# A mixture-of-experts stage: two-way softmax by tanh, router operands in PSUM, weight transposes one step later

## The chip, the cores and the metric

One core of one Trainium2 chip runs the whole kernel as one program. The metric is device time in microseconds (us) of one execution. Before the change the median of three runs is 1157.18 us (1154.05 to 1157.69).

## What is computed

The input `x` is 8 sequences of 512 tokens with 128 features, in fp32. Attention with 16 heads comes first, then a mixture of 8 experts of which each token uses 2.

```
x = layernorm(x + (x + attention(x)))
logits = x @ gate_w                              # 8 per token
top, idx = top_k(logits, 2); w = softmax(top)    # ties: the lower index wins
combine = w at idx, 0 elsewhere
h = silu(x @ w1[e]); y = h @ w2[e]
x = layernorm(x + sum over e of combine[e] * y[e])
```

## The kernel before

Every large product keeps fp32 accuracy by splitting each operand into a rounded high part and a low remainder, and adding three products (`product`: high by high, high by low, low by high).

The program is written out by hand, engine by engine: each engine has one list of instructions in a fixed order, and semaphores (`wait_ge`) tie the lists together. An engine that waits holds up all that stands behind it in its list. The attention stage is some 840 us of the span. The change lies in the expert stage behind it.

**Expert stage.** It goes through 8 sequences b ("chunks"), each with 8 steps, one per expert e; k is 8b+e. Features lie on the partitions, the 512 tokens of a sequence along the free dimension. In step e the engines do this:

- PE (TensorE): `hidden(k+3)`, 6 matmuls of 512 columns into a PSUM bank pair; `second(k)`, 6 more (L710, L714), which accumulate over the 8 experts in PSUM bank Y; `spread_c(k+3)`, one matmul (L700) that copies the routing weight of expert e over all partitions into bank CB. In step 0 the spread stands ahead of the second product. So a step is 13 matmuls.
- ACT (ScalarE): `silu_part(k+3)` (L912), then `g_hi_part(k+2)` (L919), the high part of the gated hidden values.
- DVE (VectorE): `gate_part(k+3)` (L1175), silu times the spread weight. PE's next spread waits for it, because there is one CB bank.
- POOL (GpSimd): `g_lo_part(k+2)` (L402), the low part, a subtraction of two SBUF tiles of 128x1024. `gate_part` of two steps later waits for it.

**Routing of the next sequence** runs in between. `route` (three matmuls, step 0) gives transposed logits, `logits_to_tokens` (four transposes, step 1) turns them. `route1` on DVE then copies the 32 logits of each partition (L1104), takes the maximum, subtracts it (L1109), and counts for each expert how many logits are above it, ties broken by index (L1112 to L1122). ACT takes the exponential (`exp_part`, L894). `route2` on DVE masks, sums, divides (L1128 to L1136) and so makes `combine`. `transpose_c` on PE (L681, step 3) waits for it; then ACT and DVE split the result (`cT_part`), and the first spread of the next sequence, in step 5, waits for that. All tiles of `route1` and `route2` are in SBUF but the source of the first copy.

**Normalizations.** The first one of sequence b+2 goes `to_tokens` (PE, L654, step 4), `stats1` (DVE, L1078, L1082, step 4), `rstd_part` (POOL, L396 and L398, step 5), `norm1` (DVE, L1092, step 6), `transpose_x1` (PE, L660, step 7), `x1T_part`. The second one, of sequence b-1, is `sum_part` (DVE, step 0, ahead of that step's gate): two additions over 128x512 (L1184, L1186), of which the first frees bank Y for `second` of the new sequence. Then come `sum_to_tokens` (PE, L723, step 2), `stats2_part` (DVE, step 2), `rstd_part`, and `norm2` (DVE, L1196, step 4). The first normalization works in PSUM bank NA (6), the second in NB (7), and the logits are in NB too:

```
        def nb(b):
            return COARSE + 1 if is_first(b) else NB
```

The first two and the last two chunks are written out; the four between run in a loop of two chunks.

## Time and profile before

| what | value |
|---|---|
| median of 3 runs (lowest, highest) | 1157.18 us (1154.05, 1157.69) |
| the profiled execution | 1155.28 us |
| its span, first to last instruction | 1153.5 us |
| busy share of the span | PE 92%, DVE 74%, POOL 63%, ACT 50% |
| mean granted clock of TensorE | 0.965 of 2.4 GHz |

All rows come from the one profiled execution, so costs are added against its own 1155.28 us (a span of 1153.5 and 1.8 around it). It lies 1.90 us below the median. Busy shares are means over two stages with different limits. The stage that is changed begins at about 842 us, where attention ends, and its own waits are read there. In the rows a tile has the name of the buffer that it is carved from: `probs_even` holds the small routing and normalization tiles, `x_tok` silu and gated values, `q_pair` and `k_pair` the high and low parts, `v` the transposed logits and the summed output.

### The profile page before, as it was taken

How to read it: one execution, taken by the hardware profiler on the slowest of the kernel's cores; microseconds unless marked ns; L12 is line 12 of the kernel's file. 1: busy time of each engine (PE TensorE's matmuls, PEld its weight loads, DVE VectorE, ACT ScalarE, POOL GpSimd, SP SyncE). 2: the span in 40 equal slices, each digit the busy share in tenths (PEclk: the TensorE clock that was granted, in tenths of full speed). 3: DMA queues.
4: the chain of work that ended last, by engine and by line, in shares of the span. 5: the costliest groups of instructions: out<-in, count | busy, mean ns of one | idle time of the engine just before them, and what ended most of it. 6: DMA issues, size and time to landing. Idle time of an engine off the chain costs nothing. (4 is left out here: it accounts for less than half of the span.)

```text
span 1153.5 us, 18564 instructions
## 1 busy us (share of the span) xinstructions
PE 1061.5 (92%) x5912; PEld 647.3 (56%) x5912; DVE 852.7 (74%) x1172; ACT 575.0 (50%) x680; POOL 727.1 (63%) x376
## 2 busy tenths in 40 slices
PE   4999899999999999999999999999957888889886
PEld 2555445555555555555555555556525666667664
DVE  4786778778878877877877887787735677776774
ACT  4554445455455454545545545444414565665563
POOL 0486656676666666667667666766745655666665
PEclk8899999999999999999999999999988899999999
DMA  7203012111111111111211111111000000000000
GB/s 182 78 20 110 19 42 78 46 45 59 45 45 61 62 45 45 59 45 45 77 45 45 59 46 45 50 73 46 33 27 10 10 19 12 8 18 18 9 10 19
DMA packets 41326, 52.31 MB, mean 45 GB/s; under 512 B 9296, under 2 KB 27728, under 8 KB 41296
## 3 DMA queue, kind: packets, MB, share of 16 engines
q1 hardware_dynamic: 41296, 51.92, 12.9%
q8 instruction: 17, 0.28, 0.1%
q14 instruction: 13, 0.11, 0.0%
HBM read 6.30 MB, written 2.10 MB: 7 GB/s over the span
## 5 line engine op out<-in xcount | busy, mean ns | idle before, releaser
L976 DVE TENSOR_REDUCE neg_max<-psum 128x2 fp32r<-128x1024 f32 x256 | 310.7, 1214 | 69.5 <-PE psum L507 67.0
L537 PE MATMUL psum<-q_pair,k_pair 64*128 64x512 f32 x1536 | 221.7, 393 | 3.3 <-DVE xT L958 1.9
L402 POOL TENSOR_TENSOR k_pair<-x_tok,q_pair 128x1024 fp32r<-128x1024 f32 x64 | 152.2, 2388 | 91.2 <-ACT q_pair L919 91.2
L367 POOL TENSOR_TENSOR probs_sum<-probs_sum,x_tok 128x1024 f32<-128x1024 f32 x64 | 152.6, 2384 | 72.3 <-ACT x_tok L824 69.3
L367 POOL TENSOR_TENSOR probs_sum<-probs_sum,probs_even 128x1024 f32<-128x1024 f32 x64 | 152.8, 2387 | 70.0 <-ACT probs_even L824 66.3
L824 ACT ACTIVATE probs_even<-psum 128x1024 f32<-128x1024 f32 x128 | 127.9, 1024 | 112.4 <-PE psum L543 112.4
L824 ACT ACTIVATE x_tok<-psum 128x1024 f32<-128x1024 f32 x128 | 128.3, 1025 | 110.1 <-PE psum L543 110.1
L537 PEld LDWEIGHTS psum<-q_pair,k_pair 64*128 64x128 f32 x1536 | 145.7, 186 | 32.5 <-DVE xT L958 2.4
L1175 DVE TENSOR_TENSOR x_tok<-x_tok,psum 128x1024 f32<-128x1024 f32 x64 | 77.9, 1217 | 78.2 <-PE psum L700 48.6
L555 PE MATMUL psum<-x_tok,v 128*64 128x512 f32 x512 | 132.5, 628 | 0.0
L555 PE MATMUL psum<-probs_even,v 128*64 128x512 f32 x512 | 128.4, 611 | 0.0
L507 PE MATMUL psum<-k_pair,q_pair 64*128 64x512 f32 x512 | 116.6, 450 | 10.2 <-DVE neg_max L976 10.2
L367 POOL TENSOR_TENSOR probs_sum<-probs_even 128x1024 f32<-128x1024 f32 x32 | 75.8, 2369 | 73.8 <-ACT probs_even L824 37.2
L371 POOL TENSOR_TENSOR zT_lo<-zT,zT_hi 128x512 fp32r<-128x512 f32 x64 | 83.5, 1305 | 44.7 <-ACT zT_hi L831 44.7
L1008 DVE TENSOR_TENSOR zT<-psum,zT 128x512 f32<-128x512 f32 x64 | 44.3, 692 | 87.8 <-PE psum L555 87.8
L367 POOL TENSOR_TENSOR probs_sum<-x_tok 128x1024 f32<-128x1024 f32 x32 | 75.8, 2369 | 49.0 <-DVE group_sums L992 45.8
L543 PE MATMUL psum<-shift,ones_r 64*128 64x512 f32 x512 | 102.0, 393 | 0.0
L507 PEld LDWEIGHTS psum<-k_pair,q_pair 64*128 64x128 f32 x512 | 48.6, 185 | 92.6 <-issue 54.1
L912 ACT ACTIVATE x_tok<-psum 128x1024 f32<-128x1024 f32 x64 | 65.5, 1025 | 58.0 <-PE psum L457 55.6
L831 ACT ACTIVATE zT_hi<-zT 128x512 fp32r<-128x512 f32 x64 | 40.5, 633 | 106.3 <-PE psum L457 106.2
L992 DVE TRANSPOSE_TENSOR_REDUCE group_sums<-probs_sum 128x32 f32<-128x1024 f32 x64 | 79.0, 1235 | 0.2 <-POOL probs_sum L367 0.2
L710 PE MATMUL psum<-q_pair,w_tab 128*128 128x512 f32 x256 | 72.3, 405 | 1.0 <-DVE v L1184 0.7
(117 smaller groups left out, 1836.7 us busy)
## 6 DMA issues: line engine op xcount, KB each, us to landing
xT_cur<-xT SPq DMA_DIRECT2D x32, 512.0 KB, 2.9
wqk_cur<-w_tab SPq DMA_DIRECT2D x62, 256.0 KB, 2.6
wo_cur<-w_tab SPq DMA_DIRECT2D x64, 128.0 KB, 2.0
x_tok<-L_attn_x_dram SPq DMA_DIRECT2D x8, 256.0 KB, 5.2
probs_even<-acc SPq DMA_DIRECT2D x8, 256.0 KB, 2.3
out_dram<-probs_even SPq DMA_DIRECT2D x8, 256.0 KB, 2.3
acc<-L_ffn_w_dram SPq DMA_DIRECT2D x1, 1024.0 KB, 5.7
acc<-L_attn_w_q_dram SPq DMA_DIRECT2D x1, 512.0 KB, 5.1
```

The source lines that it names most:

```text
L367: nc.gpsimd.tensor_tensor(probs_sum[:], left, probs[j][:, :, c, :], ALU.add).then_inc(s["added"], 1)
L371: nc.gpsimd.tensor_tensor(zT_lo[:], zT[:], bits(zT_hi[:]), ALU.subtract).then_inc(s["zT_lo_done"], 1)
L402: nc.gpsimd.tensor_tensor(g_lo[e % GB], gated[e % 2], bits(g_hi[e % GB]), ALU.subtract).then_inc(s["g_lo_done"], 1)
L507: mm = nc.tensor.matmul(psum[:, COARSE + h, :], q_pair[u][half, 0, t * P:(t + 1) * P], k_pair[u][half, 0, :], start=True, stop=True)
L537: nc.tensor.matmul(psum[:, 2 * (t % 2) + h, :], k_pair[u][half, kp, keys], q_pair[u][half, qp, :], start=(kp == 0 and qp == 0), stop=False)
L543: mm = nc.tensor.matmul(psum[:, 2 * (t % 2) + h, :], ones_r[half, :], shift[half].rearrange("p t q -> p (t q)"), start=False, stop=True)
L555: mm = nc.tensor.matmul(psum[h * DK:(h + 1) * DK, Z, :], v[u // 2][:, u % 2, c, h, :], probs[u % 2][:, h, c, :], start=(c == 0), stop=(c = ...
L710: nc.tensor.matmul(psum[:, Y, :], w2_tab[:, e, f, part, :], g_hi[e % GB][:, f, :], start=(e == 0 and f == 0 and part == 0), stop=False)
L824: nc.scalar.activation(probs[j][:, :, t, :], psum[:, 2 * (t % 2):2 * (t % 2) + 2, :], ACT.Exp).then_inc(s["exp_done"], 1)
L976: nc.vector.tensor_reduce(neg_max[:].rearrange("p (h k) -> p h k", h=2)[:, :, t], psum[:, COARSE:COARSE + 2, :], AX.X, ALU.max, negate=Tru ...
L992: nc.vector.tensor_reduce(group_sums[:], probs_sum[:].rearrange("p h (c i) -> p (h c) i", i=BLK), AX.X, ALU.add, apply_transpose=True).the ...
L1175: nc.vector.tensor_tensor(gated[e % 2], silu[e % 2], psum[:, CB, :].unsqueeze(1).broadcast_to([P, FC, S]), ALU.mult).then_inc(s["gated"], 1)
```

## The change

- The softmax over two chosen logits becomes `0.5 * (1 + tanh(own - (sum of both) / 2))`, and the factor 0.5 is applied where the transposed weights are split (`cT_part`). The maximum, the subtraction, the exponential, the sum of weights, the reciprocal and the division go. A mask, a sum of the two chosen logits and one combined operation (`middle`) come. ACT computes tanh.
- Logits, tie flags, counts and the tanh lie in PSUM (`log_bank`), so that no routing operation on DVE, except reductions, reads only from SBUF. The logits' bank is now NA.
- `route2` is split. Its main part stands ahead of `gate_part(5)` on DVE, the last multiplication (`route3`) behind it.
- `transpose_c` and `cT_part` go from step 3 to step 4, `to_tokens` and `stats1` from 4 to 5, `stats2_part` from 2 to 3, `norm2` from 4 to 7.
- The first addition of `sum_part` writes to bank Y itself; `second` of the new sequence now waits for `sum_done`, the end of both additions, and no longer for `sum_half`.

```diff
@@ -153,7 +153,12 @@
             return COARSE if is_first(b) else NA
         def nb(b):
-            return COARSE + 1 if is_first(b) else NB
+            return COARSE + 1 if is_first(b) else NA
+        def log_bank(b):
+            tiles = psum[:, nb(b), :].rearrange("p (t m) -> p t m", t=TT)
+            return [tiles[:, :, i * NE:(i + 1) * NE] for i in range(3)] + [tiles[:, :, NE * NE:2 * NE * NE]]
         names = """x0_in x_near_in x_far_in w_in ident_set ones_set zeroed w_split gate_split
@@ -664,8 +669,6 @@
                 pe.wait_ge(s["x1T_hi_done"], b + 1)
                 pe.wait_ge(s["x1T_lo_done"], b + 1)
-                wait(pe, s["norm2_done"], TT * (b - 2))
                 product(psum[:, nb(b), :], [gate_tab[:, 0, :], gate_tab[:, 1, :]],
                         [xT[:, b, 0, :], xT[:, b, 1, :]]).then_inc(s["logitT_done"], 1)
@@ -703,7 +706,7 @@
             def second(k, b, e):
                 if e == 0:
-                    wait(pe, s["sum_half"], b)
+                    wait(pe, s["sum_done"], b)
                 pe.wait_ge(s["g_hi_done"], k + 1)
                 for f in range(FC):
                     for part in range(2):
@@ -718,7 +721,9 @@
             def sum_to_tokens(b):
                 pe.wait_ge(s["sum_done"], b + 1)
-                wait(pe, s["logit_out"], b + 3 if not past(b, 2) else B)
+                pe.wait_ge(s["z_done"], PAIRS)
+                wait(pe, s["norm2_done"], TT * b)
                 for t in range(TT):
                     mm = nc.tensor.transpose(psum[:, NB, t * P:(t + 1) * P], sum_tok[:, t * P:(t + 1) * P], ident[:])
                 mm.then_inc(s["sum_tok_done"], 1)
@@ -768,12 +773,12 @@
                             route(b + 1)
                         if e == 1:
                             logits_to_tokens(b + 1)
-                        if e == 3:
+                        if e == 4:
                             transpose_c(b + 1)
                     if e == 2 and not is_first(b):
                         sum_to_tokens(b - 1)
                     if not past(b, 2):
-                        if e == 4:
+                        if e == 5:
                             to_tokens(b + 2)
                         if e == 7:
                             transpose_x1(b + 2)
@@ -889,21 +894,22 @@
                 wait(act, s["logit_done"], b)
                 nc.scalar.activation(logitT, psum[:, nb(b), :], ACT.Copy).then_inc(s["logitT_out"], 1)
-            def exp_part(b):
-                act.wait_ge(s["shifted"], b + 1)
-                nc.scalar.activation(expl[:], shifted[:], ACT.Exp).then_inc(s["exp_logit"], 1)
+            def tanh_part(b):
+                act.wait_ge(s["middle_done"], b + 1)
+                nc.scalar.activation(log_bank(b)[2], middle[:], ACT.Tanh).then_inc(s["tanh_done"], 1)
             def cT_part(b, j):
                 act.wait_ge(s["cT_done"], b + 1)
                 wait(act, s["cb_done"], NE * (b - 1))
-                nc.scalar.activation(cT[0:NE, j, :], psum[0:NE, na(b), :], ACT.Copy).then_inc(s["cT_hi_done"], 1)
+                nc.scalar.activation(cT[0:NE, j, :], psum[0:NE, na(b), :], ACT.Copy, scale=0.5).then_inc(s["cT_hi_done"], 1)
             zT_part(PAIRS - 2)
             x1T_part(0)
             zT_part(PAIRS - 1)
             logitT_part(0)
-            exp_part(0)
+            tanh_part(0)
             def silu_part(k, e):
                 act.wait_ge(s["h_done"], k + 1)
@@ -937,9 +943,9 @@
                     if not past(b, 1):
                         if e == 0:
                             logitT_part(b + 1)
-                        if e == 1:
-                            exp_part(b + 1)
-                        if e == 3:
+                        if e == 2:
+                            tanh_part(b + 1)
+                        if e == 4:
                             cT_part(b + 1, 1 - j)
                     if e == 7 and not past(b, 2):
                         x1T_part(b + 2)
@@ -1099,51 +1105,52 @@
             def route1(b):
+                logits, over, _, ties = log_bank(b)
+                ties = ties.rearrange("p t (a b) -> p t a b", a=NE)
                 dve.wait_ge(s["logit_done"], b + 1)
                 wait(dve, s["c_done"], b)
-                nc.vector.tensor_copy(logit[:], psum[:, nb(b), :].rearrange("p (t m) -> p t m", t=TT)[:, :, 0:NE]
-                                      ).then_inc(s["logit_out"], 1)
+                nc.vector.tensor_copy(logit[:], logits).then_inc(s["logit_out"], 1)
                 dve.wait_ge(s["logit_out"], b + 1)
-                nc.vector.tensor_reduce(top[:], logit[:], AX.X, ALU.max).then_inc(s["route_step"], 1)
-                dve.wait_ge(s["route_step"], ROUTE * b + 1)
-                nc.vector.tensor_tensor(shifted[:], logit[:], over_experts(top), ALU.subtract).then_inc(s["shifted"], 1)
-                other, own = logit[:].unsqueeze(2), logit[:].unsqueeze(3)
+                other, own = logits.unsqueeze(2), logit[:].unsqueeze(3)
                 shape = [P, TT, NE, NE]
                 nc.vector.tensor_tensor(above[:], other.broadcast_to(shape), own.broadcast_to(shape),
                                         ALU.is_gt).then_inc(s["route_step"], 1)
-                nc.vector.tensor_tensor(tied[:], other.broadcast_to(shape), own.broadcast_to(shape),
+                nc.vector.tensor_tensor(ties, other.broadcast_to(shape), own.broadcast_to(shape),
                                         ALU.is_equal).then_inc(s["route_step"], 1)
+                dve.wait_ge(s["route_step"], ROUTE * b + 2)
+                nc.vector.tensor_tensor(ties, ties, before.unsqueeze(1).broadcast_to(shape),
+                                        ALU.mult).then_inc(s["route_step"], 1)
                 dve.wait_ge(s["route_step"], ROUTE * b + 3)
-                nc.vector.tensor_tensor(tied[:], tied[:], before.unsqueeze(1).broadcast_to(shape),
-                                        ALU.mult).then_inc(s["route_step"], 1)
+                nc.vector.tensor_tensor(above[:], ties, above[:], ALU.add).then_inc(s["route_step"], 1)
                 dve.wait_ge(s["route_step"], ROUTE * b + 4)
-                nc.vector.tensor_tensor(above[:], above[:], tied[:], ALU.add).then_inc(s["route_step"], 1)
+                nc.vector.tensor_reduce(over, above[:], AX.X, ALU.add).then_inc(s["route_step"], 1)
+            def route2(b):
+                logits, over, _, _ = log_bank(b)
                 dve.wait_ge(s["route_step"], ROUTE * b + 5)
-                nc.vector.tensor_reduce(chosen[:], above[:], AX.X, ALU.add).then_inc(s["route_step"], 1)
-            def route2(b):
-                dve.wait_ge(s["route_step"], ROUTE * b + 6)
-                dve.wait_ge(s["exp_logit"], b + 1)
-                nc.vector.scalar_tensor_tensor(weight[:], chosen[:], 2.0, expl[:], ALU.is_lt,
+                nc.vector.scalar_tensor_tensor(picked[:], over, 2.0, logit[:], ALU.is_lt,
                                                ALU.mult).then_inc(s["route_step"], 1)
+                nc.vector.tensor_scalar(mask[:], over, 2.0, None, ALU.is_lt).then_inc(s["route_step"], 1)
                 dve.wait_ge(s["route_step"], ROUTE * b + 7)
-                nc.vector.tensor_reduce(wsum[:], weight[:], AX.X, ALU.add).then_inc(s["route_step"], 1)
+                nc.vector.tensor_reduce(both[:], picked[:], AX.X, ALU.add).then_inc(s["route_step"], 1)
                 dve.wait_ge(s["route_step"], ROUTE * b + 8)
-                nc.vector.reciprocal(rwsum[:], wsum[:]).then_inc(s["route_step"], 1)
-                dve.wait_ge(s["route_step"], ROUTE * b + 9)
+                nc.vector.scalar_tensor_tensor(middle[:], both[:].unsqueeze(2).broadcast_to([P, TT, NE]), -0.5, logits,
+                                               ALU.mult, ALU.add).then_inc(s["middle_done"], 1)
+            def route3(b):
+                dve.wait_ge(s["tanh_done"], b + 1)
+                dve.wait_ge(s["route_step"], ROUTE * b + 7)
                 wait(dve, s["cT_done"], b)
-                nc.vector.tensor_tensor(combine[:], weight[:], over_experts(rwsum), ALU.mult).then_inc(s["c_done"], 1)
-            ROUTE = 9
-            def over_experts(v):
-                return v[:].unsqueeze(2).broadcast_to([P, TT, NE])
+                nc.vector.scalar_tensor_tensor(combine[:], log_bank(b)[2], 1.0, mask[:], ALU.add,
+                                               ALU.mult).then_inc(s["c_done"], 1)
+            ROUTE = 8
             def cT_part(b, j):
                 dve.wait_ge(s["cT_hi_done"], b + 1)
-                nc.vector.tensor_tensor(cT[CLO:CLO + NE, j, :], psum[0:NE, na(b), :], bits(cT[0:NE, j, :]),
-                                        ALU.subtract).then_inc(s["cT_lo_done"], 1)
+                nc.vector.scalar_tensor_tensor(cT[CLO:CLO + NE, j, :], psum[0:NE, na(b), :], 0.5, bits(cT[0:NE, j, :]),
+                                               ALU.mult, ALU.subtract).then_inc(s["cT_lo_done"], 1)
             dve.wait_ge(s["gate_in"], DMA)
@@ -1166,6 +1173,7 @@
             route1(0)
             route2(0)
             stats1(1)
+            route3(0)
             def gate_part(k, e):
                 dve.wait_ge(s["silu_done"], k + 1)
@@ -1181,9 +1189,9 @@
                 dve.wait_ge(s["y_done"], NE * (b + 1))
                 wait(dve, s["sum_tok_done"], b)
-                nc.vector.tensor_tensor(sum_tok, psum[:, Y, :], bits(xT[:, b, 0, :]), ALU.add).then_inc(s["sum_half"], 1)
+                nc.vector.tensor_tensor(psum[:, Y, :], psum[:, Y, :], bits(xT[:, b, 0, :]), ALU.add).then_inc(s["sum_half"], 1)
                 dve.wait_ge(s["sum_half"], b + 1)
-                nc.vector.tensor_tensor(sum_tok, sum_tok, bits(xT[:, b, 1, :]), ALU.add).then_inc(s["sum_done"], 1)
+                nc.vector.tensor_tensor(sum_tok, psum[:, Y, :], bits(xT[:, b, 1, :]), ALU.add).then_inc(s["sum_done"], 1)
             def stats2_part(b):
                 norm_stats(NB, stats2, mv2, b, "sum_tok_done", "stats2_done", "mv2_done", ("norm2_done", TT))
@@ -1210,22 +1218,24 @@
                         sum_part(b - 1)
                         if not past(b, 1):
                             x1T_part(b + 1)
+                    if not past(b, 1) and e == 2:
+                        route2(b + 1)
                     if not last_step(b, e + 3):
                         gate_part(b * NE + e + 3, (e + 3) % NE)
                     if not past(b, 1):
                         if e == 1:
                             route1(b + 1)
                         if e == 2:
-                            route2(b + 1)
-                        if e == 3:
+                            route3(b + 1)
+                        if e == 4:
                             cT_part(b + 1, 1 - j)
                     if not is_first(b):
-                        if e == 2:
+                        if e == 3:
                             stats2_part(b - 1)
-                        if e == 4:
+                        if e == 7:
                             norm2(b - 1)
                     if not past(b, 2):
-                        if e == 4:
+                        if e == 5:
                             stats1(b + 2)
                         if e == 6:
                             norm1(b + 2)
```

DVE, second chunk, from the last operation of `route1` (step 1) to the gate behind the split of the weights. L1175 is `gate_part`, L1145 `cT_part`, L1078 and L1082 the statistics. Before:

```order
L1122 TENSOR_REDUCE probs_even<-probs_even 128x32
L1175 TENSOR_TENSOR x_tok<-x_tok,psum 128x1024
L1128 SCALAR_TENSOR_TENSOR probs_even<-probs_even 128x32
L1131 TENSOR_REDUCE probs_even<-probs_even 128x4
L1133 RECIPROCAL probs_even<-probs_even 128x4
L1136 TENSOR_TENSOR probs_even<-probs_even 128x32
L1078 BN_STATS probs_even<-psum 128x6 x4
L1082 BN_AGGR probs_even<-probs_even 128x2 x4
L1175 TENSOR_TENSOR x_tok<-x_tok,psum 128x1024
L1145 TENSOR_TENSOR xT_cur<-psum,xT_cur 8x512
```

The same place in the changed kernel (L1183 is `gate_part`, L1152 `cT_part`, L1145 `route3`, L1084 and L1088 the statistics):

```order
L1126 TENSOR_REDUCE psum<-probs_even 128x4x8
L1132 SCALAR_TENSOR_TENSOR probs_even<-psum,probs_even 128x32
L1134 TENSOR_SCALAR probs_even<-psum 128x32
L1136 TENSOR_REDUCE probs_even<-probs_even 128x4
L1138 SCALAR_TENSOR_TENSOR probs_even<-probs_even,psum 128x32
L1183 TENSOR_TENSOR x_tok<-x_tok,psum 128x1024
L1145 SCALAR_TENSOR_TENSOR probs_even<-psum,probs_even 128x32
L1183 TENSOR_TENSOR x_tok<-x_tok,psum 128x1024
L1084 BN_STATS probs_even<-psum 128x6 x4
L1088 BN_AGGR probs_even<-probs_even 128x2 x4
L1183 TENSOR_TENSOR x_tok<-x_tok,psum 128x1024
L1152 SCALAR_TENSOR_TENSOR xT_cur<-psum,xT_cur 8x512
```

Four small operations moved ahead of the gate of step 2, one stays behind it, and the statistics and the weight split each stand one gate later.

DVE, in the loop, from the gates of steps 6 and 7 to the sum of the finished sequence in step 0 of the next chunk (L1092 is `norm1`; L1184 and L1186 are the two additions). Before:

```order
L1175 TENSOR_TENSOR x_tok<-x_tok,psum 128x1024
L1088 ISA
L1092 TENSOR_SCALAR probs_even<-psum,probs_even 128x128 x4
L1171 REGISTER_ALU
L1175 TENSOR_TENSOR x_tok<-x_tok,psum 128x1024
L1181 REGISTER_ALU
L1184 ISA
L1184 TENSOR_TENSOR v<-psum,xT 128x512
L1186 ISA
L1186 TENSOR_TENSOR v<-v,xT 128x512
```

And now (L1098 is `norm1`, L1204 `norm2`, L1192 and L1194 the additions):

```order
L1098 TENSOR_SCALAR probs_even<-psum,probs_even 128x128 x4
L1179 REGISTER_ALU
L1183 TENSOR_TENSOR x_tok<-x_tok,psum 128x1024
L1200 ISA
L184 REGISTER_ALU
L1204 TENSOR_SCALAR probs_even<-psum,probs_even 128x128 x4
L1192 ISA
L1192 TENSOR_TENSOR psum<-psum,xT 128x512
L1194 ISA
L1194 TENSOR_TENSOR v<-psum,xT 128x512
```

The four operations of the second normalization now stand between the last gate of a chunk and the two additions.

ACT, second chunk, around the exponential (L894) and the tanh (L899). Before, and then now:

```order
L912 ACTIVATE x_tok<-psum 128x1024
L919 ACTIVATE q_pair<-x_tok 128x1024
L894 ACT_TABLE_LOAD
L894 ACTIVATE probs_even<-probs_even 128x32
L912 ACT_TABLE_LOAD
```

```order
L918 ACTIVATE x_tok<-psum 128x1024
L925 ACTIVATE q_pair<-x_tok 128x1024
L899 ACTIVATE psum<-probs_even 128x4x8
L918 ACTIVATE x_tok<-psum 128x1024
L925 ACTIVATE q_pair<-x_tok 128x1024
```

The two table loads around the exponential have gone, and none stands at the tanh, which comes one step later.

## Rows read from the trace of the kernel before

**Rows 1.** The page, section 2: granted clock in 40 equal slices
```profile
PEclk8899999999999999999999999999988899999999
```
**Rows 2.** Waits from 825 us to the end (us in total, times, longest)
```profile
PE psum L681 <- DVE probs_even L1136: 28.8, 8, 4.0
```
**Rows 3.** Timeline of PE: start, us, line, operands, count, [idle before <-releaser]
```profile
950.58 0.60 PE L660 MATMUL psum<-ident,probs_even 128*128 128x128 f32 x4
...
952.71 0.50 PE L700 MATMUL psum<-xT_cur,w_tab 128*128 128x512 f32 x1
953.38 1.19 PE L710 MATMUL psum<-q_pair,w_tab 128*128 128x512 f32 x4 [0.18 <-DVE v L1184]
...
958.97 0.60 PE L675 MATMUL psum<-ident,v 128*128 128x128 f32 x4
...
962.41 0.60 PE L723 MATMUL psum<-ident,v 128*128 128x128 f32 x4
...
970.42 0.69 PE L681 MATMUL psum<-ident,probs_even 128*8 128x128 f32 x4 [3.97 <-DVE probs_even L1136]
...
975.45 0.60 PE L654 MATMUL psum<-ident,probs_even 128*128 128x128 f32 x4
...
1087.87 0.60 PE L660 MATMUL psum<-ident,probs_even 128*128 128x128 f32 x4
```
**Rows 4.** Timeline of DVE, routing of one chunk
```profile
960.46 0.18 DVE L1104 COPY probs_even<-psum 128x32 f32<-128x32 f32 x1
...
964.67 1.22 DVE L1175 TENSOR_TENSOR x_tok<-x_tok,psum 128x1024 f32<-128x1024 f32 x1 [0.59 <-ACT x_tok L912]
965.81 2.25 DVE L1128 SCALAR_TENSOR_TENSOR probs_even<-probs_even 128x32 f32<-128x32 f32 x1
...
968.53 1.83 DVE L1136 TENSOR_TENSOR probs_even<-probs_even 128x32 f32<-128x32 f32 x1
```
**Rows 5.** Timeline of POOL at the same time
```profile
965.67 4.65 POOL L402 TENSOR_TENSOR k_pair<-x_tok,q_pair 128x1024 fp32r<-128x1024 f32 x2 [3.67 <-ACT q_pair L919]
```
**Rows 6.** Line L1128, all eight: ns min/median/max
```profile
L1128 DVE SCALAR_TENSOR_TENSOR probs_even<-probs_even x8: 193/2257/2264, 871.0 to 1102.8; 128x32 f32<-128x32 f32 x8
```
**Rows 7.** Busy time and granted clock (after the five engines' columns) in four stretches
```profile
93.50:97.00 3.50, 3.50 (x13) 1.74 (x13) 0.00 (x0) 1.97 (x2) 0.63 (x1) 0.51 0.00 0
...
148.00:151.50 3.50, 3.50 (x14) 0.98 (x12) 3.02 (x5) 0.60 (x1) 2.35 (x1) 0.53 0.00 0
...
936.00:941.00 5.00, 4.92 (x17) 3.92 (x18) 2.99 (x11) 2.41 (x3) 1.20 (x2) 0.66 0.00 0
941.00:950.00 9.00, 9.00 (x43) 7.32 (x42) 6.97 (x19) 4.95 (x6) 7.08 (x5) 1.00 0.19 60
```
**Rows 8.** Groups by line and form from 840 us: the table loads ahead of silu
```profile
L912 ACT ACT_TABLE_LOAD x8 | 10.3, 1283 | 0.1
```
**Rows 9.** Timeline of DVE: second normalization of a chunk, and the chunk's end
```profile
942.48 1.36 DVE L1196 TENSOR_SCALAR probs_even<-psum,probs_even 128x128 f32<-128x128 f32 x4
...
951.43 1.22 DVE L1175 TENSOR_TENSOR x_tok<-x_tok,psum 128x1024 f32<-128x1024 f32 x1 [1.10 <-POOL k_pair L402]
952.57 0.68 DVE L1184 TENSOR_TENSOR v<-psum,xT 128x512 f32<-128x512 f32 x1
953.40 0.80 DVE L1186 TENSOR_TENSOR v<-v,xT 128x512 f32<-128x512 f32 x1
```
**Rows 10.** Timeline of PE: three shorter idle stretches in the attention stage
```profile
92.60 0.39 PE L455 MATMUL psum<-w_tab,xT_cur 128*128 128x256 f32 x1 [2.46 <-DMA xT_cur<-xT]
...
117.55 0.96 PE L537 MATMUL psum<-q_pair,k_pair 64*128 64x512 f32 x6 [1.27 <-DVE recip L998]
...
146.72 0.50 PE L507 MATMUL psum<-k_pair,q_pair 64*128 64x512 f32 x2 [2.30 <-DVE neg_max L976]
```
**Rows 11.** Timeline of PE: the weight transposes of the first sequence
```profile
871.95 0.60 PE L681 MATMUL psum<-ident,probs_even 128*8 128x128 f32 x4 [0.93 <-DVE probs_even L1136]
```
**Rows 12.** Timeline of DVE: statistics of the second sequence, just behind its weights
```profile
871.81 0.88 DVE L1078 BATCH_NORM_STATS2 probs_even<-psum 128x6 f32<-128x128 f32 x4
```

8 lines of the change are left out of this document (4 added, 4 removed).

## The prediction

> **What bounds the kernel now.** I read the granted clock by slices first [rows 1]. It is at its upper level through attention and falls at the start and around the expert stage, so TensorE loses something there. Attention is not touched by the change; everything is decided in the last 310 us. The waits of that stage name one culprit: PE waits 8 times at the transposes of the routing weights (L681), 28.8 us in all, for DVE's last routing operation (L1136) [rows 2]. Seven of these are alike, near 4 us each; the first one is 0.93 us [rows 11], so the seven hold 27.9 us.
>
> The timeline of PE shows one of them [rows 3]. From the transposes at 958.97 to those at 962.41 are 3.44 us, and that is one full step with its four transposes and next to no waiting. From 962.41 to 970.42, with the same content, are 8.01 us, and from 970.42 to 975.45 are 5.03 us. The first excess, 4.57 us, is the wait (3.97) and a short one ahead of it; the second, 1.59 us, has no idle time. There the clock is low: 0.66 as a mean in the matching stretch of the chunk before, and 1.00 right behind it [rows 7], which are the 1.2 and 2.4 GHz levels mixed. So each wait costs a chunk of 34.3 us (four of them between 950.58 and 1087.87 [rows 3]) 4.57 + 1.59 = **6.16 us**. No other engine sets a chunk: POOL needs 8 products of 2.4 us and some 2.5 us more.
>
> Why is DVE late? L1128 works on 32 elements per partition and takes 2.25 us, and L1136 takes 1.83 [rows 4]. Over all eight, L1128 ranges from 193 to 2264 ns [rows 6]. The long ones lie beside POOL's two subtractions, 965.67 to 970.32 [rows 5], and end as a POOL operation ends: 965.81 + 2.25 is 968.06, 968.53 + 1.83 is 970.36. Both read two tiles in SBUF. The gate (L1175), also beside them elsewhere, reads one tile in SBUF and one in PSUM and keeps 1.22 us.
>
> **The change, part by part.**
>
> *The weights come in time.* Before, `route1` and the wait behind it fill 960.46 to 964.67, of which 0.59 is a wait for ACT [rows 4]; so `route1` is at most 3.6 us, and it loses two operations of eight. The four operations that now stand ahead of the gate are priced by the shortest L1128, 0.19 us, with the gaps 0.22 each: 0.9 us [rows 6]. The gate then starts between 963.8 and 965.0, against 964.67 before: 0.9 earlier to 0.3 later. The last operation stands behind it and needs 0.2, if it doesn't wait for POOL: `combine` is ready by 966.4. The transposes, now one step later, want it at about 966.2 + 3.4 = 969.6. More than 3 us of slack, so both excesses go, in seven chunks: 7 x 6.16 = **43.1 us gained**. What is late next in this chain is the split of the weights, ahead of the first spread of the next sequence: ACT 0.6 and DVE 0.7 behind the transposes, with a whole hidden and second product (2.8) before the spread wants it. I cost it at nothing.
>
> *Table loads.* The order shows 14 of them gone behind the first silu, of 1283 ns each [rows 8]. They made the 0.59 us wait of the gate [rows 4], which is in the 4.57 already. ACT otherwise idles for PE. Nothing more is gained.
>
> *PSUM operands.* As a source, PSUM costs DVE nothing here: L1184 with one source in PSUM takes 0.68 us, L1186 with both in SBUF 0.80 [rows 9]. As a destination of DVE it has no row. Below, it can't gain over the bare time. Above, if it doubled the operation, three operations of `route1` (some 0.4 each, of which about 0.5 is covered by the slack of the gate) and the first addition (0.7) would cost 0.7 + 0.7 us a chunk, 10 us in all. The nearest row is the 0.68 of a PSUM source; I take 0 and keep 10 for the upper end.
>
> *The sum at the chunk's end.* This is what the change pays with. Before, the last gate of a chunk starts at 951.43, the first addition follows at 952.57, and `second` of the new sequence starts at 953.38, 1.95 us after the gate's start [rows 3, 9]. Now `norm2` stands between, four operations that take 1.3 us in a row (1.36 [rows 9]), and `second` waits for both additions, 0.7 more. It starts 1.95 + 1.3 + 0.7 = 3.95 us after the gate's start. The gate itself waited 1.10 us in all for POOL [rows 9], whose reciprocal root stands in the same place still; 0 to 1.1 could be won, I take 0.4, and 0.3 more since the low part of the first normalization, for which PE waits behind `second`, is then done. That is 2.0 - 0.4 - 0.3 = 1.3 us at five boundaries, 2.0 at the last one (no POOL wait there), and 0.3 at the first, where no `norm2` stands yet: 5 x 1.3 + 2.0 + 0.3 = **8.8 us lost**.
>
> *The clock at that place.* PE's spread ends by 952.6 to 952.9 (it starts at 952.71 at the latest [rows 3]), and `second` would start at 951.43 - 0.4 + 3.95 = 955.0. PE is idle for 2.1 to 2.4 us at six boundaries. The trace has two stretches like it: 2.46 and 2.30 us idle [rows 10]. PE resumed at full clock both times, and 1 us later the clock fell: 0.51 in 93.5 to 97.0 and 0.53 in 148.0 to 151.5 [rows 7]. An idle stretch of 1.27 us [rows 10] was followed by matmuls at their usual rate. Each fall costs half of 3.5 us, 1.7, and PE is what bounds the chunk: 6 x 1.7 = **10.2 us lost**. The Trainium skill, "TensorE: Matmul & The Clock Gate", section "Why this matters for your kernels", advises to keep idle gaps below about 3 us and takes the clock to last through shorter ones. These rows speak against it; by the skill this term would be 0 and the time 10.2 us shorter.
>
> *The first sequence.* There its `combine` is finished behind the statistics of the second one, which take 0.88 us and their four aggregates; before, they stood behind [rows 12]. `route1` gets shorter too. Between 0.93 us won (that wait gone [rows 11]) and 1.3 lost, I take **0.8 lost**, as the statistics alone cost 0.88.
>
> *The tail.* `norm2` of the last but one sequence moves by three steps in which DVE has only gates, and POOL's last products still set the end. Nothing.
>
> *Sum:* 43.1 - 8.8 - 10.2 - 0.8 = 23.3 us. Against the profiled execution's 1155.28 us this gives 1132.0. The median of before is 1.9 us above it, the lowest run 1.2 below, so I keep **1132 us**.
>
> **The rivals.**
>
> 1. *The clock stays up at the boundary.* It is the skill's rule of the paragraph above, and rows of 1.27 us idle time [rows 10] show it for shorter stretches. A gate that starts earlier than I take would help it. Against it stand two out of two stretches of 2.3 and 2.5 us. Then the gain is 33.5 and the time 1122 us. Chance 0.18.
> 2. *No stall at the boundary at all*, if the last gate came so much earlier that `norm2` and the additions fit. They need 3.95 us after the gate, and PE has 1.2 us of spread and slack; it speaks strongly against. Gain 42, time 1113 us. Chance 0.04.
> 3. *PSUM destinations are dear.* Up to 10 us as worked out, 1142 us. Nothing in the rows speaks for it but that no row shows the operation. Chance 0.13.
> 4. *Slower than before: the routing block ahead of the gate.* Ten small operations now stand in front of `gate_part` of step 2, and PE's next spread waits for that gate. It has about 0.5 us of slack. If the block were X longer than that, PE would lose X in seven chunks and, from 2 us on, 1.7 more by the clock. To eat 23.3 us and pass the 0.3% it takes 27 = 7 x (X + 1.7), so X above 2.1 us: each of the ten operations 0.26 us longer than now. The bare 193 ns of L1128 [rows 6] speak against it. At X = 3 the time would be 1132 + 33 = 1165 us. Chance 0.03.
> 5. *Something else holds the chunk at 34 us*, so that the wait was hidden. The step from 958.97 to 962.41 takes 3.44 us without it, and POOL's load is below 22 us a chunk. About 1155 us; chance 0.03. That the change doesn't do what it says is excluded for the table loads and the order of DVE, which are read from the program; that PSUM sources keep DVE clear of POOL is shown by the gate.
>
> **How the numbers follow.** The forecast, 1132, has 0.59. Its own range is 1126 to 1138: the gate's start (0.4 between 0 and 1.1 at six boundaries, about 4 us), the first sequence (1 to 2 us), and one or two clock falls more or less. The range reaches to rival 1 with its own few us and most of the way to rival 3: **1118 to 1141 us**. A measurement tells this kernel from no change at about 0.3%, 3.5 us. Faster by more than that: 0.94; within it: 0.03; slower: 0.03.
>
> **What would show it.** In the new profile no wait of PE at the transposes of the weights, and the routing operations at their bare 0.2 and 0.4 us beside POOL. Chunks of 31 to 31.5 us. Seven waits of PE at `second` for DVE's second addition, six of 2.1 to 2.4 us, each followed by some 3.5 us at half clock. If chunks take 29.5 and the clock is at 1.00 in them, rival 1 is right; if they take 28 or less and that wait is missing, rival 2; if DVE's operations into PSUM last 0.8 us, rival 3. A wait of PE at the spread of step 3 for the gate, of over a microsecond, would be rival 4.

## The result, and the profile after the change

| | before | changed |
|---|---|---|
| median | 1156.33 us (1154.05 to 1157.69, 4 runs) | 1127.24 us (1123.37 to 1129.15, 4 runs) |
| the profiled execution | 1155.28 us | 1129.15 us |
| its span | 1153.5 us | 1127.4 us |
| mean granted clock of TensorE | 0.965 | 0.975 |

The ratio is 0.9746, with a 95% interval of 0.9715 to 0.9778: 29 us faster. The changed kernel's profiled execution is its slowest one, 1.9 us above its median, as before's lay 1 us below. A second set of runs, beside two of the experiments, gave 0.9787 (0.9771 to 0.9804), so the gain is 24 to 29 us. One of the four runs of the kernel with the exponential, below, took 1679 us at a mean granted clock of 0.565 and is left out of its median.

The waits of the expert stage first, in the view that [rows 2] come from, here from 825 us to the end of the changed kernel (us in total, times, longest):

```profile
PE psum L713 <- DVE v L1194: 14.2, 7, 2.3
...
PEld psum L684 <- DVE probs_even L1145: 1.8, 1, 1.8
...
PE psum L684 <- DVE probs_even L1145: 1.6, 1, 1.6
```

The seven waits of 4 us at the transposes of the weights (now L684) are gone, and the first sequence's alone is left (1.6 us). In their place PE waits seven times at the first matmul of `second` (L713) for DVE's second addition (L1194), 14.2 us in all: six of 2.1 to 2.3 us and, at the first boundary, one of 0.83. The timeline of PE, start and duration in us, shows one chunk with two of these boundaries; these rows answer to [rows 3]:

```profile
938.54 0.39 PE L703 MATMUL psum<-xT_cur,w_tab 128*128 128x512 f32 x1
941.22 1.18 PE L713 MATMUL psum<-q_pair,w_tab 128*128 128x512 f32 x4 [2.29 <-DVE v L1194]
...
957.91 0.60 PE L684 MATMUL psum<-ident,probs_even 128*8 128x128 f32 x4
...
961.35 0.60 PE L659 MATMUL psum<-ident,probs_even 128*128 128x128 f32 x4
...
972.34 1.43 PE L713 MATMUL psum<-q_pair,w_tab 128*128 128x512 f32 x4 [2.29 <-DVE v L1194]
```

From 957.91 to 961.35 are 3.44 us, where the same content took 5.03 before. From 941.22 to 972.34 is one chunk: 31.12 us, before 34.3. The clock, in the view of [rows 7] (the granted clock stands behind the five engines' columns):

```profile
930.00:941.00 11.00, 8.93 (x43) 6.98 (x41) 8.61 (x21) 7.31 (x8) 9.07 (x7) 1.00 0.03 10
941.00:942.00 1.00, 0.79 (x3) 0.67 (x4) 1.00 (x3) 0.00 (x0) 1.00 (x1) 1.00 0.87 288
942.50:946.00 3.50, 3.50 (x10) 2.75 (x9) 0.31 (x1) 0.60 (x1) 0.75 (x1) 0.53 0.02 5
946.00:957.00 11.00, 11.00 (x54) 8.96 (x53) 7.21 (x18) 6.66 (x8) 6.30 (x3) 1.00 0.01 1
```

Here PE resumes at 2.4 GHz (granted clock 1.00 up to 942), and within a microsecond or so it falls to 1.2 GHz for about 3.5 us. At 1034.58 and 1065.46 the clock is at 0.50 already when PE resumes. DVE around the routing block, the same view as [rows 4]:

```profile
949.47 0.18 DVE L1112 COPY probs_even<-psum 128x32 f32<-128x32 f32 x1
949.69 0.42 DVE L1116 TENSOR_TENSOR probs_even<-psum,probs_even 128x256 f32<-128x256 f32 x1
950.03 0.42 DVE L1118 TENSOR_TENSOR psum<-psum,probs_even 128x256 f32<-128x256 f32 x1
...
951.42 0.43 DVE L1126 TENSOR_REDUCE psum<-probs_even 128x32 f32<-128x256 f32 x1
951.88 0.19 DVE L1132 SCALAR_TENSOR_TENSOR probs_even<-psum,probs_even 128x32 f32<-128x32 f32 x1
...
952.20 0.19 DVE L1136 TENSOR_REDUCE probs_even<-probs_even 128x4 f32<-128x32 f32 x1
952.42 0.19 DVE L1138 SCALAR_TENSOR_TENSOR probs_even<-probs_even,psum 128x32 f32<-128x32 f32 x1
952.62 1.22 DVE L1183 TENSOR_TENSOR x_tok<-x_tok,psum 128x1024 f32<-128x1024 f32 x1
953.76 0.18 DVE L1145 SCALAR_TENSOR_TENSOR probs_even<-psum,probs_even 128x32 f32<-128x32 f32 x1
```

POOL's subtractions run from 948.60 to 951.01 and from 952.05 to 954.45 beside most of them, and none is longer for it: not those with one source in PSUM, and not the reduction L1136 (0.19 us), which reads one tile only, in SBUF. A PSUM destination costs nothing: L1118 writes to PSUM and takes 0.42, as L1116, which writes to SBUF. And the boundary, the view of [rows 9]:

```profile
937.14 1.22 DVE L1183 TENSOR_TENSOR x_tok<-x_tok,psum 128x1024 f32<-128x1024 f32 x1 [0.69 <-POOL k_pair L407]
938.28 1.36 DVE L1204 TENSOR_SCALAR probs_even<-psum,probs_even 128x128 f32<-128x128 f32 x4
939.56 0.69 DVE L1192 TENSOR_TENSOR psum<-psum,xT 128x512 f32<-128x512 f32 x1
940.39 0.69 DVE L1194 TENSOR_TENSOR v<-psum,xT 128x512 f32<-128x512 f32 x1
```

`second` starts at 941.22, 4.08 us after the gate's start at 937.14 (forecast: 3.95). The four rows are, in order, what PE waits for: the gate, the normalization, and the two additions.

### The profile page after: what moved, and what is told of

It is laid out like the page before. It is cut to its first block, busy times and chain, and to the rows that moved or that the text cites. A ratio compares the mean times of both kernels' runs of the same rounds, so it can differ in the third digit from the quotient of the medians.

```text
span 1127.4 us, 18513 instructions
## 1 busy us (share of the span) xinstructions
PE 1053.1 (93%) x5912; PEld 647.2 (57%) x5912; DVE 816.1 (72%) x1164; ACT 557.6 (49%) x666; POOL 727.9 (65%) x376
## 4 chain that ended last, share of the span: by engine, by line
PE 76%; POOL 10%; issue 6%; DVE 4%; ACT 1%; DMA 1%; SPq 1%; POOLq 0%; DVEq 0%; ACTq 0%
PE psum L560 21%; PE psum L542 15%; PE psum L460 9%; POOL k_pair L407 8%; PE psum L512 7%; PE psum L461 6%; PE psum L462 6%; PE psum L548 5%; PE psum L713 2%; PE psum L520 1%; PE psum L717 1%; POOL probs_even L403 1%; DMA xT_cur<-xT 1%; DVE neg_max L982 1%; PE psum L574 0%
## 5 line engine op out<-in xcount | busy, mean ns | idle before, releaser
L1183 DVE TENSOR_TENSOR x_tok<-x_tok,psum 128x1024 f32<-128x1024 f32 x64 | 78.1, 1220 | 88.1 <-PE psum L703 68.2
L713 PE MATMUL psum<-q_pair,w_tab 128*128 128x512 f32 x256 | 73.9, 412 | 14.2 <-DVE v L1194 14.2
```

The lines of the kernel that those rows point to most:

```text
L713: nc.tensor.matmul(psum[:, Y, :], w2_tab[:, e, f, part, :], g_hi[e % GB][:, f, :], start=(e == 0 and f == 0 and part == 0), stop=False)
```

## The experiments

Each ratio is to the kernel before, run beside it on the same chip, with its 95% interval. "The changed kernel" has 0.9746 and 0.9787 in its two sets. The change made three things at once: operands in PSUM, a softmax by tanh, and a new order with a new wait. They are taken apart here.

### What the boundary costs: norm2 in step 4 again

In DVE's list, of the changed kernel:

```diff
                     if not is_first(b):
                         if e == 3:
                             stats2_part(b - 1)
-                        if e == 7:
+                        if e == 4:
                             norm2(b - 1)
```

> The changed kernel with norm2 back in step 4, so that it no longer stands between a chunk's last gate and the two additions. My theory (the additions come late because of norm2, PE idles 2.3 us, and the clock falls behind it): PE's idle time at the second product of a new sequence shrinks by 1.3 us, from 2.3 to 1.0 us, the clock no longer falls there, and six boundaries give 6 x (1.3 + 1.7) = 18 us: about 1109 us. Rival A (the clock falls there for another reason than this stretch): 6 x 1.3 = 8 us, about 1119 us, with the half-clock stretches still there. Rival B (DVE or POOL is what spaces the chunk, the time comes back elsewhere): under 3 us.

Measured: ratio 0.9625 (0.9605 to 0.9646), median 1111.18 us, 14 to 19 us faster than the changed kernel. PE at three boundaries:

```profile
939.86 1.19 PE L713 MATMUL psum<-q_pair,w_tab 128*128 128x512 f32 x4 [1.02 <-DVE v L1194]
...
968.13 1.20 PE L713 MATMUL psum<-q_pair,w_tab 128*128 128x512 f32 x4 [1.03 <-DVE v L1194]
...
996.39 1.19 PE L713 MATMUL psum<-q_pair,w_tab 128*128 128x512 f32 x4 [1.00 <-DVE v L1194]
```

The idle stretch is 1.0 us, a chunk 28.27 us. That is 2.85 us less, of which 1.27 is idle time; the other 1.58 has no idle time ahead of it. The clock shows it, which is 1.00 over 100 us of this kernel (the view of [rows 7]):

```profile
900.00:1000.00 100.00, 96.11 (x448) 77.01 (x447) 70.36 (x162) 62.51 (x70) 77.22 (x43) 1.00 0.06 19
```

So both terms of the forecast's loss are real: without the long stretch its idle time and the half clock behind it are both gone. Rivals A and B fall. The changed kernel's second trace (`changed_again`, below) gives the price of a fall without any edit. There the clock fell at five of the six boundaries, and at one it did not:

```profile
940.01 1.19 PE L713 MATMUL psum<-q_pair,w_tab 128*128 128x512 f32 x4 [2.27 <-DVE v L1194]
...
969.54 1.37 PE L713 MATMUL psum<-q_pair,w_tab 128*128 128x512 f32 x4 [2.29 <-DVE v L1194]
```

```profile
940.00:950.00 10.00, 9.99 (x47) 8.21 (x48) 5.81 (x14) 4.68 (x6) 5.18 (x3) 1.00 0.12 39
...
970.50:974.00 3.50, 3.50 (x10) 2.69 (x10) 0.64 (x1) 0.60 (x1) 1.07 (x1) 0.53 0.07 28
```

The chunk without the fall is 29.53 us, the next one, with it, 31.14 (969.54 to 1000.68): 1.6 us, at the same idle time.

### The same from the other side: the sum as it was

```diff
-                    wait(pe, s["sum_done"], b)
+                    wait(pe, s["sum_half"], b)
...
-                nc.vector.tensor_tensor(psum[:, Y, :], psum[:, Y, :], bits(xT[:, b, 0, :]), ALU.add).then_inc(s["sum_half"], 1)
+                nc.vector.tensor_tensor(sum_tok, psum[:, Y, :], bits(xT[:, b, 0, :]), ALU.add).then_inc(s["sum_half"], 1)
                 dve.wait_ge(s["sum_half"], b + 1)
-                nc.vector.tensor_tensor(sum_tok, psum[:, Y, :], bits(xT[:, b, 1, :]), ALU.add).then_inc(s["sum_done"], 1)
+                nc.vector.tensor_tensor(sum_tok, sum_tok, bits(xT[:, b, 1, :]), ALU.add).then_inc(s["sum_done"], 1)
```

> The changed kernel with the sum as it was before: the first addition writes to SBUF and frees the PSUM bank, the second product waits for it alone; norm2 stays in step 7. Theory: the idle stretch shrinks by 0.7 us, from 2.3 to 1.6 us, at six boundaries and from 0.8 to 0.1 at the first: 5 us, about 1122 us, if the clock still falls behind 1.6 us; if it stays up, 10 us more, about 1112 us. Rival: the second addition, now of two SBUF tiles again, waits for POOL and delays x1T_part and the gate behind it, so that the gain is under 2 us.

Measured: ratio 0.9651 (0.9632 to 0.9669), median 1113.63 us. The boundary of two chunks:

```profile
937.42 1.19 PE L713 MATMUL psum<-q_pair,w_tab 128*128 128x512 f32 x4 [1.46 <-DVE v L1192]
...
966.29 1.19 PE L713 MATMUL psum<-q_pair,w_tab 128*128 128x512 f32 x4 [1.46 <-DVE v L1192]
```

The stretch is 1.46 us and a chunk 28.87 us; the clock is 1.00 from 900 to 1000 us. It is 0.83 us less idle time and 1.42 us less besides. An edit that is worth 0.8 us a chunk on DVE gave 2.25, because no fall of the clock followed the shorter stretch at any of the six boundaries.

### Both

> The changed kernel with both: norm2 in step 4 and the second product waiting for the first addition alone. Theory: the idle stretch goes from 2.3 to 0.3 us, the clock stays up, six boundaries give 6 x (2.0 + 1.7) = 22 us and the first 0.7: about 1105 us. Rival (once the stretch is short enough for the clock, the rest is hidden): no better than norm2 early alone.

Measured: ratio 0.9611 (0.9593 to 0.963), median 1109.48 us, 2 us better than norm2 early alone. The theory's 1105 was too good, and the timeline of PE shows a good part of why:

```profile
937.58 1.20 PE L713 MATMUL psum<-q_pair,w_tab 128*128 128x512 f32 x4 [0.18 <-DVE v L1192]
939.62 0.49 PE L460 MATMUL psum<-xT,wqk_cur 128*128 x1 [0.38 <-DVE xT L1103]
...
965.65 1.19 PE L713 MATMUL psum<-q_pair,w_tab 128*128 128x512 f32 x4 [0.18 <-DVE v L1192]
```

The wait at `second` is down to 0.18 us, but a new one of 0.38 us stands right behind it, at `route`, for the low part of the first normalization (`x1T_part`, L1103), which DVE does after both additions. A chunk is 28.07 us, 0.20 less than with norm2 early alone, where 0.84 of idle time had gone. So 0.38 of the 0.64 us that are missing is this wait, which had been hidden behind the first one; the other 0.26 has no idle time that the trace shows.

### And x1T_part between the two additions

```diff
                 nc.vector.tensor_tensor(sum_tok, psum[:, Y, :], bits(xT[:, b, 0, :]), ALU.add).then_inc(s["sum_half"], 1)
+                between()
                 dve.wait_ge(s["sum_half"], b + 1)
...
-                        sum_part(b - 1)
-                        if not past(b, 1):
-                            x1T_part(b + 1)
+                        if past(b, 1):
+                            sum_part(b - 1)
+                        else:
+                            sum_part(b - 1, lambda: x1T_part(b + 1))
```

> The kernel with norm2 early and the second product waiting for the first addition, with the low part of the first normalization (x1T_part) put between the two additions. Theory: PE's remaining wait behind the second product (0.36 us for x1T_part, some 0.3 more until matmuls run on) goes, 0.3 to 0.6 us in six chunks: 2 to 4 us less than the 1109 of both_early. Rival (the second addition, of two SBUF tiles, then meets POOL and delays the gate): no gain.

Measured: ratio 0.959 (0.957 to 0.961), median 1106.95 us, the lowest of the study. Its interval is clear of the kernel before's and the changed one's, but overlaps that of the last section (0.9593 to 0.963), so it is the chunk that shows the gain. PE's transposes of the sum, once a chunk, come every 27.4 us:

```profile
948.20 0.60 PE L728 MATMUL psum<-ident,v 128*128 128x128 f32 x4
...
975.64 0.60 PE L728 MATMUL psum<-ident,v 128*128 128x128 f32 x4
```

That is 0.63 us a chunk (28.07 to 27.44) below the kernel of the last section, at the upper end of what was expected. By my estimate a chunk without any wait needs 27.0 us: 8 steps of 3.02 us (954.89 to 957.91 of the changed kernel), five sets of transposes at 0.42 (3.44 less 3.02) and the three matmuls of `route`, 0.7. So little is left.

### The operands back in SBUF

Of the changed kernel, its order, tanh and waits kept:

```diff
         def log_bank(b):
-            tiles = psum[:, nb(b), :].rearrange("p (t m) -> p t m", t=TT)
-            return [tiles[:, :, i * NE:(i + 1) * NE] for i in range(3)] + [tiles[:, :, NE * NE:2 * NE * NE]]
+            return sb_bank
...
+        sb_bank = [logit[:], carve(TT, NE), carve(TT, NE), carve(TT, NE * NE)]
```

> The changed kernel with logits, flags, counts and tanh in SBUF again, the transposes in step 4. Theory: the operations with two SBUF sources wait for POOL's subtraction again. In the block ahead of the gate of step 2 that costs 1 to 4 us, the gate comes late, PE waits for it at the spread and not at the transposes, 0.5 to 3.5 us a chunk and a clock fall with the longer ones: ratio to before 0.98 to 1.00. Rival (the order is what counts, the transposes have 3 us of slack in step 4): ratio as the changed kernel, 0.972 to 0.977.

Measured: ratio 0.9959 (0.9938 to 0.998), median 1152.33 us. Nearly all of the gain is gone. DVE and PE:

```profile
992.58 1.68 DVE L1116 TENSOR_TENSOR probs_even<-probs_even 128x256 f32<-128x256 f32 x1
994.18 0.41 DVE L1118 TENSOR_TENSOR probs_even<-probs_even 128x256 f32<-128x256 f32 x1
...
995.09 2.65 DVE L1124 TENSOR_TENSOR probs_even<-probs_even 128x256 f32<-128x256 f32 x1
...
998.96 1.22 DVE L1183 TENSOR_TENSOR x_tok<-x_tok,psum 128x1024 f32<-128x1024 f32 x1
```

```profile
984.19 1.19 PE L713 MATMUL psum<-q_pair,w_tab 128*128 128x512 f32 x4 [2.31 <-DVE v L1194]
1000.23 0.50 PE L703 MATMUL psum<-xT_cur,w_tab 128*128 128x512 f32 x1 [2.45 <-DVE x_tok L1183]
```

Two operations of the same shape as L1118 take 1.68 and 2.65 us in place of 0.41. POOL's subtractions run from 991.58 to 993.98 and from 995.04 to 997.46 beside them. The gate behind them starts at 998.96, and PE's spread waits 2.45 us for the gate. The transposes don't wait, except the first sequence's (3.5 us). This is the place of rival 4 of the prediction, with another cause than it named.

With the transposes in step 3 as well (the same edit as in the next section):

> The same with operands in SBUF and the transposes in step 3. Theory: as the run before, plus the wait at the transposes wherever the last operation waits for POOL: slower than sbuf_step4 by 0 to 15 us. Rival (PSUM operands bring nothing): the same as c_step3.

Measured: ratio 0.9978 (0.9962 to 0.9993), median 1152.59 us, no different from the last one beyond the intervals. PE waits for the gate at the same spread there (18.4 us in all), and again not at the transposes, but for the first sequence's; the extra wait that was expected did not come.

### The transposes back in step 3, PSUM kept

On PE, ACT and DVE:

```diff
-                        if e == 4:
+                        if e == 3:
                             transpose_c(b + 1)
...
-                        if e == 4:
+                        if e == 3:
                             cT_part(b + 1, 1 - j)
```

> The changed kernel with the transposes of the routing weights and their split back in step 3 (PSUM operands and the early part of the routing kept). Theory: in the changed kernel the last routing operation ends 1.1 us before PE would come to the transposes even in step 3, so nothing waits and the later step is worth nothing by itself: the ratio to before stays at 0.972 to 0.977. Rival (the later step brought the gain): PE waits 4 us again at the transposes in 7 chunks and the time is that of before.

Measured: ratio 0.9753 (0.9722 to 0.9785), median 1127.32 us. There is no wait at the transposes but the first sequence's, 1.5 us. The time is that of the changed kernel within the intervals, so the later step brought none of the gain that can be told from noise. It may be worth a little: in this trace PE waits 0.27 us more at the last spread of a chunk, and a chunk with the clock up is 30.12 us (940.32 to 970.44) where the changed kernel's was 29.53. But the clock fell at only four of the six boundaries of this execution, which hides up to 3 us.

### The kernel before, with the later step alone

Transposes and split in step 4, `to_tokens` and `stats1` in step 5, as in the diff of the change, and nothing else.

> The kernel before with only the schedule moved: transposes of the weights and their split in step 4, to_tokens and stats1 in step 5, nothing else. Theory: L1136 ends at the same time, some 4 us late for step 3, which is 0.6 us late for step 4: PE waits 0.6 us in 7 chunks in place of 4.0 and the clock stays up, 7 x (3.4 + 1.6) = 35 us gained less 0 to 5 us at the boundary: ratio 0.97 to 0.975, without the dear boundary of the changed kernel. Rival (DVE's blocked operations delay the gates as well, and that bounds the chunk): under 20 us gained.

Measured: ratio 0.9969 (0.9952 to 0.9986), median 1151.7 us. My theory's number fell, and the rival held: 4 us gained where I expected 30 to 35. The timeline of PE:

```profile
970.68 0.49 PE L700 MATMUL psum<-xT_cur,w_tab 128*128 128x512 f32 x1 [3.67 <-DVE x_tok L1175]
971.02 0.60 PE L681 MATMUL psum<-ident,probs_even 128*8 128x128 f32 x4
```

The 4 us wait has moved by one instruction. The transposes don't wait any more, and the spread ahead of them waits 3.67 us for the gate, since that gate stands in DVE's list behind the same blocked operations. I had looked at who waits for L1136 only, and not at what is queued behind it: here the gate starts at 969.41, behind both blocked operations. Moving one reader of a blocked DVE operation later doesn't help while another one's work stands in the same list.

### The kernel before, with the operands in PSUM alone

Exponential, table loads, order and sum of before kept; logits in bank NA:

```diff
-                nc.vector.tensor_tensor(shifted[:], logit[:], over_experts(top), ALU.subtract).then_inc(s["shifted"], 1)
+                nc.vector.tensor_tensor(shifted[:], logits, over_experts(top), ALU.subtract).then_inc(s["shifted"], 1)
...
-                nc.vector.scalar_tensor_tensor(weight[:], chosen[:], 2.0, expl[:], ALU.is_lt,
+                nc.vector.scalar_tensor_tensor(weights, over, 2.0, expl[:], ALU.is_lt,
...
-                nc.vector.tensor_tensor(combine[:], weight[:], over_experts(rwsum), ALU.mult).then_inc(s["c_done"], 1)
+                nc.vector.tensor_tensor(combine[:], weights, over_experts(rwsum), ALU.mult).then_inc(s["c_done"], 1)
```

`weights`, `over` and the ties are tiles of `log_bank`, as in the changed kernel.

> The kernel before, its softmax by the exponential and its whole order kept (transposes in step 3, norm2 in step 4, sum as it was), with the logits in bank NA and the flags, counts and weights in PSUM, so that no routing operation has two SBUF sources. Theory (DVE's operations that wait for POOL are what held the chunk): the last routing operation then ends 1 us after PE has come to the transposes, PE waits 0 to 1 us there in place of 4.0, the clock stays up there and no boundary gets dearer: 30 to 42 us gained, 1113 to 1125 us, as good as the changed kernel or better. Rival (the tanh, with fewer operations and no table loads, or the new order is needed too): under 20 us gained.

Measured: ratio 0.9624 (0.9601 to 0.9646), median 1109.66 us. Beside it, on the same chip:

> The changed kernel once more beside the other two on the same chip: ratio 0.972 to 0.978 to the kernel before. It tells whether before_psum differs from it.

Measured: ratio 0.9787 (0.9771 to 0.9804), median 1128.38 us. So the operands in PSUM alone are worth 43 us, all that the wait at the transposes cost, and the changed kernel is 19 us slower than the kernel with PSUM operands alone. That kernel's last routing operations:

```profile
950.20 0.19 DVE L1135 SCALAR_TENSOR_TENSOR psum<-psum,probs_even 128x32 f32<-128x32 f32 x1
...
950.87 0.19 DVE L1143 TENSOR_TENSOR probs_even<-psum,probs_even 128x32 f32<-128x32 f32 x1
```

They answer to L1128 and L1136 of [rows 4], 0.19 each in place of 2.25 and 1.83. Its chunk is 28.3 us.

### The exponential in place of the tanh

`ACT.Tanh` becomes `ACT.Exp` in the changed kernel. Its routing weights are then wrong; every expert is computed for every token all the same, so its time can be compared.

> The changed kernel with the exponential in place of the tanh (the routing weights are then not those of the softmax), which brings back two table loads a chunk around it, 1.28 us each. Theory: ACT has that time, and the tables were worth next to nothing: the next silu ends up to 1.3 us later, the gate behind it up to 1.3 us, of which PE has some 0.5 us slack: 0 to 5 us slower, about 1129 us. Rival (the table loads gave a good part of the gain): 2 x 1.3 us in each of 7 chunks, 15 us or more slower.

Measured: ratio 0.9815 (0.9794 to 0.9837), median 1133.04 us, 3 to 8 us slower than the changed kernel. ACT of one chunk:

```profile
951.13 1.28 ACT L899 ACT_TABLE_LOAD   x1
952.42 0.20 ACT L899 ACTIVATE psum<-probs_even 128x32 f32<-128x32 f32 x1
952.64 1.28 ACT L918 ACT_TABLE_LOAD   x1
```

Two loads a chunk come back, and a chunk takes 1.1 to 1.3 us more. The expectation said 0 to 5 us; in the changed order the loads are not quite free, and the tanh is worth some 5 us there. Seven such chunks would be 8 us; the clock fell at four of the six boundaries only in this trace, which takes some 3 us off. In the kernel with PSUM operands alone the loads are present too, and it is as fast (1109.66 us, chunks of 28.3) as `both_early`, which has the tanh and the boundary of before (1109.48, chunks of 28.07). In that order the tanh is worth 0.2 us a chunk, which the times don't show.

## Why the prediction was right, point by point

The range and the direction held: 1127.24 us, forecast 1132, and the gain, 29 us by the medians and 26.1 by the two profiled executions, was forecast as 23.3. I go through its steps on the two profiled executions, from the first `to_tokens` (846.13 before, 847.47 changed) to the end: 307.4 us before, 279.9 changed, 27.4 gained (the attention stages differ by 1.3 the other way, which is no part of the change).

- **"The weights come in time", 6.16 us a chunk.** Right. The step behind the transposes is 3.44 us now, the two ahead of them are 6.49 (951.42 to 957.91; one has transposes of its own), and the kernel with PSUM alone gains 43 us, as 7 x 6.16 did. The step from there to the cause, that operations with two SBUF sources wait for POOL, was right too: four kernels (PSUM or SBUF, step 3 or 4) follow the operands and ignore the step. But the text took its slack ("more than 3 us") from the later step, which was not needed. And it did not see that the gate stands behind the same blocked operations, so that the later step alone could not have brought the gain: 4 us in the kernel before with that step alone.
- **"The sum at the chunk's end", 1.3 us a boundary.** Right: 4.08 us from gate to `second`, forecast 3.95, and the gate's wait for POOL was 0.69 in place of 1.10, so 0.4 was won there, as taken.
- **"The clock at that place", 1.7 us.** Right in its size: 1.6 us between two chunks of one trace, and 1.4 and 1.6 us a chunk beyond the idle time when the stretch was shortened. That it came at all six boundaries, as forecast, was in part luck: with stretches of the same 2.1 to 2.3 us the clock fell at 6 of 6 in this execution, at 5 of 6 in `changed_again`, and at 4 of 6 each in the kernels with the transposes in step 3 and with the exponential. The forecast had "one or two clock falls more or less" in its range only. So the advice of the Trainium skill, "TensorE: Matmul & The Clock Gate", section "Why this matters for your kernels", to avoid gaps above about 3 us, was not enough here: 19 of these 24 shorter ones were followed by half clock. Together the three terms made a chunk 3.16 us shorter; 124.24 us for four chunks (941.22 to 1065.46) against 137.24 (953.38 to 1090.62) is 3.25 each.
- **"The first sequence", 0.8 us lost.** From `to_tokens` of the second sequence to the first transposes it was 1.54 us before and 2.16 now, 0.6 lost. But ahead of it the stretch of 2.08 us that ends at 865.22 went with no fall of the clock in this execution, while before, one of 2.09 us that ends at 864.86 did. That is 1.6 us that no step of mine had, and not a part of the change. From the transposes of the weights to the first `second` of the next sequence, chunk 0 got 6.9 us shorter, forecast 5.9. These two make 2.6 of the 4 us that the forecast was short of the 27.4; the rest is 0.1 us a chunk and the like.
- **"Table loads. Nothing more is gained."** Right for the sum: a chunk came out at the forecast's length. But the loads would not have been free in the changed order, where they cost 1.1 to 1.3 us a chunk beside the exponential; the prediction took them as worth only the gate's 0.59 us wait. In the order of before it is 0.2 us.
- **"The tail. Nothing."** Right: from the last `second` of a first expert to the end it is 1.8 us longer, which is the clock behind the last boundary.
- **Rivals.** 1 fell as a rule for the kernel, but came true at single boundaries: the chunk of 29.53 us with the clock at 1.00 is the very sign that was named for it. 2 fell: the wait at `second` is there. 3 fell: 0.42 us into PSUM. 5 fell: a chunk is 31.12 us. 4 did not come true with PSUM operands, but its path (block, gate, spread) is just what happened with SBUF operands and in the kernel with the later step alone.

One thing the prediction did not ask is whether the change's parts were all worth having. They were not: PSUM operands 43 us won, the later `norm2` and the wait for both additions 14 to 20 us lost, the later transposes next to nothing either way, and the tanh saved some 5 us that the table loads would have cost in the changed order.

## What to carry to other kernels

When a tiny DVE operation takes microseconds, look at what POOL does at that moment and at how many of its sources lie in SBUF; moving one source to PSUM is a better cure than moving the reader later, because all that stands behind the operation in DVE's list is late too. Before work is put into an engine's last slot of a pipeline stage, add up what the next stage's first instruction waits for. And where TensorE bounds a kernel, price an idle stretch of 2.1 to 2.3 us at some 1.6 us above its length, since the clock fell at 19 of 24 such boundaries here; a stretch of 1.0 to 1.5 us once a chunk cost only itself. Since the falls don't come every time, compare kernels by chunks with the same clock, and not by the median alone, when a few microseconds are in question.

## What was not expected of the hardware

- PE's idle stretches of 1.0 us (norm2 early) and 1.46 us (the sum as it was), once a chunk, were followed by full clock every time, those of 2.1 to 2.3 us by half clock, mostly for about 3.5 us, at 19 of 24 boundaries in four traces. Once, with the transposes in step 3, the half clock lasted over 5 us (from before 970.4 to past 976), and that chunk took 32.91 us. The length of the stretch alone doesn't decide it: with SBUF operands four stretches of 2.41 to 2.45 us (966.26, 1000.23, 1034.17, 1068.14) were followed by full clock, and so was one of 3.59 us in the kernel before with the later step (1106.57), while in every trace of a kernel with the tanh and PSUM operands two stretches of 1.56 and 1.61 us close together (871.34 and 873.55 in the changed one) went with a fall. What decides stays open.
- DVE's operations on 256 elements with one source and the destination in PSUM took 0.42 us, the same shape in SBUF 0.41 us when POOL was idle and up to 2.65 us when it was not. That POOL's instruction ends it was read from the ends of both in the kernel before; whether a POOL instruction of another kind would do the same was not tried. DVE's operations that read one SBUF tile only were not held up: L1136 of the changed kernel, 0.19 us beside POOL.
- The tanh runs with the tables of silu loaded: one table load stands in the whole expert stage of the changed kernel, against 15 before.
